# An attention kernel on TensorE: context matmuls of 256 columns, one head each, and the heads of the g tensors 64 bytes further apart in SBUF

## The chip, the cores and the metric

The kernel runs on one core of one Trainium2 chip. The metric is the device time of one execution in microseconds (us), the median of three runs. SBUF is the on-chip memory of 128 partitions from which TensorE reads both operands of a matmul; PSUM is the one that it writes.

## The reference

Cross attention with 8 heads over 8 batches, 256 queries, 256 keys and head width 256, then a projection, a residual and a layer norm:

```python
Q = (img_embed @ Wq).reshape(B, -1, H, D).transpose(0, 2, 1, 3)
K = (sent_embed @ Wk).reshape(B, -1, H, D).transpose(0, 2, 1, 3)
V = (sent_embed @ Wv).reshape(B, -1, H, D).transpose(0, 2, 1, 3)
score = jnp.einsum('bhqd,bhkd->bhqk', Q, K) / math.sqrt(D)
score = jnp.where(mask, score, -jnp.inf)
attn = jax.nn.softmax(score, axis=-1)
ctx = jnp.einsum('bhqk,bhkd->bqhd', attn, V).reshape(B, -1, H * D)
out = ctx @ Wo + img_embed
# then (out - mean) / sqrt(var + 1e-05) * gamma + beta over the last axis
```

`img_embed` is x (8, 256, 256) and `sent_embed` is ctx_768 (8, 256, 192), both float32.

## The kernel before, in words

Once, at the start, the weights are folded per head: A = Wq Wk^T (256 x 192, `fold_A`, L324) and C = Wv Wo (192 x 256, `fold_C`, L341). Scores are then x A ctx^T, and the output is the sum over heads of (attn ctx) C. The 192 context features are split in a lower part of 128 (tensors with L) and an upper part of 64 (U); the upper parts of two heads share one tile of 128 partitions.

Every product on TensorE is made of float32r matmuls on operands split in two: a hi part (the value rounded to float32r by ScalarE, `hi_part`) and a lo part (the rest, by VectorE or GpSimd, `lo_part`); the products hi*hi, hi*lo and lo*hi are accumulated in PSUM.

The work goes in 32 steps (8 batches of 4 head pairs; `t` is the step, `j` the pair, `b` the batch). TensorE's own order in one step (`step`, L501) is:

1. `scores(t)`, L383: 20 matmuls of 256 columns, head 0's ten and then head 1's ten. Stationary operand: a 128-column slice of `gL_hi`, `gL_lo` or `gU`; moving operand: `ctxT_hi` or `ctxT_lo`.
2. `query_products(t + 1)`, L365: 18 of 256 columns. Stationary `A_hi`, `A_lo`; moving `xT_hi`, `xT_lo`. They fill `gU_bank` and `gL_bank`, from which ScalarE and VectorE make the g tensors of the next step.
3. `output_products(t - 4)`, L458 to L499: 18 of 256 columns. Stationary `tL_hi`, `tL_lo`, `tU_hi`, `tU_lo`; moving `CL_*`, `CU_*`.
4. `context_products(t - 3)`, L420: 10 matmuls of 512 columns, both heads in one. Stationary `ctxL_hi`, `ctxL_lo`, `ctxU`; moving `pT_hi`, `pT_lo` (the transposed probabilities).

Each matmul has a weight load of its own (LDWEIGHTS) ahead of it, also where the next one uses the same stationary slice. Steps 6 to 29 run in a hardware loop of four steps; the others are written out. In the first steps, in which there is nothing yet for parts 3 and 4, `fold_C` stands in their place. In the last steps the order is written out by hand: the probabilities of steps 30 and 31 are transposed on TensorE (`transposes`, L405), and step 30 keeps its t tensors elsewhere (`places`, L133): tL in `xT_hi`/`xT_lo`, tU in the two halves of `gU`.

All engines work from in-order queues. ScalarE takes the exponentials and the hi parts, VectorE the row maxima, lo parts and 32x32 transposes, GpSimd the normalisation and the lo part of pT, SyncE the DMAs. Semaphores tie them together: `g_hi_done` and `g_split` release the scores, `pT_hi_done` and `pT_split` the context phase, `t_product` (raised when tL and when tU are complete) releases ScalarE's `t_hi_part`.

**Where the operands lie.** SBUF tensors are laid one behind the other in the order in which the program declares them, each rounded up to 32 bytes per partition. Up to `tU_lo` all sizes are multiples of 256 bytes, and the first tensor starts at a multiple of 128. Then come `eps_col` and `power_col` (8 bytes each, 32 taken), then the g tensors, xT, ctxT, C and pT. So, in bytes modulo 128, A, ctxL, ctxU, tL and tU start at 0, and gL, gU, xT, ctxT, CL, CU and pT at 64. Slices of 128 columns are 512 bytes long, and every slice that a matmul reads starts a multiple of 256 bytes into its tensor.

Of the kernel before, what the change touches and what calls it, by code (L numbers as in the profile page):

```python
# [8 lines left out]
F32R = mybir.dt.float32r  # L9
# [4 lines left out]
P = 128  # L14
B = 8
S = 256
# [12 lines left out]
KT = KV // P  # L29
# [7 lines left out]
SQ = 32  # L37
SQUARES = KV // SQ
ROWS = P // SQ

def attention_kernel(nc, xT, x, ctxT, ctx, mask, wqT, wkT, wvT, wo, gamma, beta, out, scratch):
    es = ExitStack()
    with es:
        def sb(name, shape, dt=F32):
            return es.enter_context(nc.sbuf_tensor(name, shape, dt))
# [14 lines left out]
        ctxL_hi = sb("ctxL_hi", [P, KT, P], F32R)  # L60
# [7 lines left out]
        eps_col = sb("eps_col", [P, QT])  # L68
        power_col = sb("power_col", [P, QT])

        gL_hi = sb("gL_hi", [P, 2, S], F32R)
        gL_lo = sb("gL_lo", [P, 2, S], F32R)
        gU = sb("gU", [P, 2, S], F32R)

        xT_hi = sb("xT_hi", [P, IT, S], F32R)
        xT_lo = sb("xT_lo", [P, IT, S], F32R)
# [239 lines left out]
        def _(pe):  # L316
            def split_products(into, pairs, first=True, last=True, shared=False):

                for n, (stationary, moving) in enumerate(pairs):
                    ins = nc.tensor.matmul(into, stationary, moving, start=first and n == 0,  # L320
                                           stop=last and n == len(pairs) - 1, skip_group_check=shared)
                return ins
# [97 lines left out]
            def context_products(t, j, b):  # L420

                if j == 0:

                    pe.wait_ge(C_split, 2 * (PAIRS - 1))

                    pe.wait_ge(ctx_split, 2 * b + 2)
                hi, lo, tL, tU = pT_hi[j % 2], pT_lo[j % 2], places("tL", t)[0], places("tU", t)[0]

                pe.wait_ge(pT_hi_done, 2 * t + 2)
                if isinstance(t, int) and t == STEPS - 1:  # L430

                    split_products(tU[:], [(ctxU[:, k, :], hi[:, k]) for k in range(KT)], last=False)
                    pe.wait_ge(pT_split, 2 * t + 2)
                    split_products(tU[:], [(ctxU[:, k, :], lo[:, k]) for k in range(KT)],
                                   first=False).then_inc(t_product, 1)
                    split_products(tL[:], [pair for k in range(KT) for pair in
                                           [(ctxL_hi[:, k, :], hi[:, k]), (ctxL_lo[:, k, :], hi[:, k]),
                                            (ctxL_hi[:, k, :], lo[:, k])]]).then_inc(t_product, 1)
                    return
                split_products(tL[:], [(part[:, k, :], hi[:, k]) for k in range(KT) for part in (ctxL_hi, ctxL_lo)],  # L440
                               last=False)

                if isinstance(t, int) and STEPS - 4 <= t < STEPS - 2:

                    pe.wait_ge(tU_summed, 2 * t)
                split_products(tU[:], [(ctxU[:, k, :], hi[:, k]) for k in range(KT)], last=False)
                by_squares = not (isinstance(t, int) and t >= STEPS - 2)
                for k in range(KT):

                    pe.wait_ge(pT_split, 2 * t + (k + 1 if by_squares else 2))  # L450
                    end = k == KT - 1
                    lower = split_products(tL[:], [(ctxL_hi[:, k, :], lo[:, k])], first=False, last=end)
                    if end:
                        lower.then_inc(t_product, 1)
                    upper = split_products(tU[:], [(ctxU[:, k, :], lo[:, k])], first=False, last=end)
                upper.then_inc(t_product, 1)

            def output_lower(t, j, b, q):  # L458
# [665 lines left out]
```

## Time and profile before

| | |
|---|---|
| median of three runs | 319.12 us (319.02 to 319.21) |
| the profiled execution | 319.14 us |
| its span, first to last instruction | 317.3 us |
| matmuls recorded | 2264 |
| PE (matmul) busy | 309.8 us |
| PEld (weight load) busy | 290.7 us |
| VectorE (DVE) busy | 253.0 us |
| ScalarE (ACT) busy | 221.9 us |
| GpSimd (POOL) busy | 181.2 us |
| mean granted TensorE clock | 0.998 of full speed |

The profile and its trace are of one execution. Engines are named as in the table. Matmuls overlap in the pipeline, so the duration of one (0.28 us for 256 columns) is longer than what it takes of the engine's time; that is read from the distance between the starts of consecutive matmuls, here called the pitch. The timeline has starts to 0.01 us, so a pitch is taken over many matmuls. L320 is the line of the helper `split_products` that issues all matmuls of the four phases; the phases are told apart by their tiles.

### The profile page before, as it was taken

To read this page: it belongs to the slowest core of one execution; us is meant where nothing else is said; L and a number is where in the kernel's file an instruction comes from. 1 tells how busy PE (TensorE), PEld (TensorE's weight loads), DVE (VectorE), ACT (ScalarE), POOL (GpSimd) and SP (SyncE) were. 2 spreads that over 40 slices of the span, in tenths; PEclk is the share of its full clock that TensorE was granted. 3 is DMA by queue.
4 is the path that set the end of the run, shared out by engine and by line. 5 is a ranking of instruction groups with operands and counts; after the bars stand their busy time and mean duration, and the time that the engine had idled before them with its cause. 6 is when DMAs were issued, how large, how long until landed. Compare 5 with 4: busy or idle time off the path is not lost.

```text
span 317.3 us, 7411 instructions
## 1 busy us (share of the span) xinstructions
PE 309.8 (98%) x2264; PEld 290.7 (92%) x2264; DVE 253.0 (80%) x721; ACT 221.9 (70%) x601; POOL 181.2 (57%) x183
## 2 busy tenths in 40 slices
PE   8899999999999999999999999999999999999993
PEld 7898888999999999999999999999999999999982
DVE  0466778777999879987998889987998889975686
ACT  2446677768867787678777797678767887777640
POOL 1123476457864587558855586558755686457312
PEclk9999999999999999999999999999999999999999
DMA  7995443464344553484446444364356435440101
GB/s 257 365 409 219 136 155 130 141 211 136 99 146 169 189 166 121 140 243 136 132 128 198 156 154 158 131 215 150 115 190 180 169 101 186 144 138 20 35 0 66
DMA packets 46910, 50.26 MB, mean 158 GB/s; under 512 B 3504, under 2 KB 37040, under 8 KB 46896
## 3 DMA queue, kind: packets, MB, share of 16 engines
q1 hardware_dynamic: 46608, 49.56, 47.2%
q10 hardware_dynamic: 288, 0.52, 0.6%
q8 instruction: 7, 0.11, 0.2%
q14 instruction: 7, 0.06, 0.1%
HBM read 32.24 MB, written 17.83 MB: 158 GB/s over the span
## 4 chain that ended last, share of the span: by engine, by line
PE 93%; DMA 2%; DVE 2%; ACT 1%; SPq 1%; issue 0%; POOLq 0%; POOL 0%; DVEq 0%
PE score_bank L320 25%; PE out_bank L320 19%; PE gL_bank L320 14%; PE tL_bank L320 13%; PE tU_bank L320 9%; PE gU_bank L320 7%; DMA wq_raw<-in_wqT 2%; PE spare_bank L354 1%; PE tL_bank L354 1%; PE spare_bank L320 1%; PE tL_bank L336 1%; PE tU_bank L336 1%; PE out_bank L360 1%; PE tU_bank L360 1%; DVE tU L827 1%; PE out_bank L336 0%
## 5 line engine op out<-in xcount | busy, mean ns | idle before, releaser
L1003 POOL TENSOR_TENSOR probs<-probs,inv_sum 128x512 f32<-128x512 f32 x64 | 66.6, 1041 | 85.5 <-DVE inv_sum L790 84.9
L601 ACT ACTIVATE probs<-neg_scores,neg_max 128x256 f32<-128x256 f32 x128 | 64.2, 503 | 35.5 <-DVE neg_max L779 35.4
L1026 POOL TENSOR_TENSOR pT_lo<-pT_raw,pT_hi 128x512 fp32r<-128x512 f32 x60 | 76.5, 1297 | 8.6 <-ACT pT_hi L558 8.6
L779 DVE CUSTOM_DVE_ANT_0 neg_scores<-score_bank,mask_bias 128x256 f32<-128x256 f32 x128 | 49.1, 420 | 6.5 <-PE score_bank L320 4.0
L800 DVE STREAM_TRANSPOSE squares<-probs 128x512 f32<-128x512 f32 x60 | 42.3, 706 | 0.5 <-DMA scratch<-squares 0.2
L558 ACT ACTIVATE tL_hi<-tL_bank 128x512 fp32r<-128x512 f32 x31 | 18.5, 598 | 31.5 <-PE tL_bank L320 31.5
L320 PE MATMUL score_bank<-ctxT_hi,gU 128*128 128x256 f32 x128 | 36.5, 285 | 0.0
L727 DVE TENSOR_TENSOR tL_lo<-tL_bank,tL_hi 128x512 fp32r<-128x512 f32 x31 | 21.4, 689 | 18.8 <-ACT tL_hi L558 18.8
L320 PE MATMUL score_bank<-ctxT_hi,gL_lo 128*128 128x256 f32 x128 | 36.2, 283 | 0.0
L320 PE MATMUL score_bank<-ctxT_hi,gL_hi 128*128 128x256 f32 x128 | 36.2, 283 | 0.0
L320 PE MATMUL score_bank<-ctxT_lo,gL_hi 128*128 128x256 f32 x128 | 36.2, 283 | 0.0
L320 PE MATMUL score_bank<-ctxT_lo,gU 128*128 128x256 f32 x128 | 36.2, 283 | 0.0
L320 PE MATMUL gL_bank<-xT_hi,A_hi 128*128 128x256 f32 x128 | 35.3, 276 | 0.0
L320 PE MATMUL gL_bank<-xT_lo,A_hi 128*128 128x256 f32 x128 | 35.3, 276 | 0.0
L320 PE MATMUL gL_bank<-xT_hi,A_lo 128*128 128x256 f32 x128 | 35.3, 276 | 0.0
L558 ACT ACTIVATE pT_hi<-pT_raw 128x512 fp32r<-128x512 f32 x60 | 34.3, 622 | 0.0
L320 PE MATMUL out_bank<-CL_lo,tL_hi 128*128 128x256 f32 x118 | 32.6, 276 | 0.0
L320 PE MATMUL out_bank<-CL_hi,tL_hi 128*128 128x256 f32 x118 | 32.6, 276 | 0.0
L320 PE MATMUL out_bank<-CL_hi,tL_lo 128*128 128x256 f32 x118 | 32.6, 276 | 0.0
L727 DVE TENSOR_TENSOR gU<-gU_bank,gU 64x256 fp32r<-64x256 f32 x64 | 27.0, 423 | 2.1
L827 DVE TENSOR_TENSOR tU<-tU_bank,tU_moved 64x256 f32<-64x256 f32 x62 | 26.0, 419 | 1.6 <-ACT tU_moved L642 0.6
L320 PEld LDWEIGHTS score_bank<-ctxT_hi,gU 128*128 128x128 f32 x128 | 24.4, 191 | 2.6 <-issue 1.2
(167 smaller groups left out, 946.8 us busy)
## 6 DMA issues: line engine op xcount, KB each, us to landing
scratch<-squares SPq DMA_DIRECT2D x30, 512.0 KB, 2.7
pT_raw<-scratch SPq DMA_DIRECT2D x120, 128.0 KB, 3.1
xT_raw<-in_xT SPq DMA_DIRECT2D x8, 256.0 KB, 4.5
ctxT_raw<-in_ctxT SPq DMA_DIRECT2D x8, 256.0 KB, 4.7
wo_raw<-in_wo SPq DMA_DIRECT2D x4, 512.0 KB, 13.7
x_res<-in_x SPq DMA_DIRECT2D x8, 256.0 KB, 3.2
out<-y_out SPq DMA_DIRECT2D x7, 256.0 KB, 2.8
wq_raw<-in_wqT SPq DMA_DIRECT2D x3, 512.0 KB, 7.6
```

The source lines that it names most:

```text
L320: ins = nc.tensor.matmul(into, stationary, moving, start=first and n == 0, stop=last and n == len(pairs) - 1, skip_group_check=shared)
L336: ins = nc.tensor.matmul(dst[:, i * DL:(i + 1) * DL], wq_raw[:, h * DT + d, i * P:(i + 1) * P], wk_raw[:, h * DT + d, :], start=d == 0, st ...
L354: ins = nc.tensor.matmul(lower[:, hh, :], wv_raw[:, h * DT + d, 0:P], wo_raw[:, h * DT + d, :], start=d == 0, stop=d == DT - 1)
L360: ins = nc.tensor.matmul(upper[hh * UP:(hh + 1) * UP, 0, :], wv_raw[:, h * DT + d, P:DL], wo_raw[:, h * DT + d, :], start=d == 0, stop=d = ...
L558: return nc.scalar.activation(dst, src, ACT.Copy)
L601: nc.scalar.activation(probs[j % 2][:, n, :], neg_scores[:, n, :], ACT.Exp, bias=neg_max[:, n:n + 1], scale=-1.0, accum_out=row_sum[:, n:n ...
L727: return nc.vector.tensor_tensor(dst, whole, hi.bitcast(F32), ALU.subtract)
L779: nc.vector.tensor_tensor_reduce(out=neg_scores[:, n, :], in0=score_bank[hh][:, q, :], in1=mask_bias[:], scale=-SCALE, scalar=3.0e38, op0= ...
L800: nc.vector.transpose(squares[:, :, rows, :].rearrange("p s n c -> p n s c"), probs[j % 2][:, rows, :].rearrange("p n (s c) -> p n s c", c ...
L827: nc.vector.tensor_tensor(tU[part, :], places("tU", t)[0][part, hh, :], tU_moved[part, :], ALU.add).then_inc(tU_summed, 1)
L1003: nc.gpsimd.tensor_tensor(probs[j % 2][:, rows, :], probs[j % 2][:, rows, :], inv, ALU.mult) \
L1026: nc.gpsimd.tensor_tensor(pT_lo[j % 2][:, k].rearrange("p hh (q i r) -> p (hh q) i r", q=QT, i=ROWS), pT_raw[j % 2][:, k].rearrange("p i n ...
```

## The change

The g tensors get 16 float32 of padding behind each head, so that head 1 starts 1088 instead of 1024 bytes behind head 0, and each of the three takes 128 bytes more. And the context phase issues for each (stationary, moving) pair two matmuls of 256 columns, one for each head, instead of one of 512. The two write their own halves of the PSUM bank; only the first of a bank carries the start flag. Order of pairs, waits and semaphore increments are as before.

```diff
+APART = 16
@@
-        gL_hi = sb("gL_hi", [P, 2, S], F32R)
-        gL_lo = sb("gL_lo", [P, 2, S], F32R)
-        gU = sb("gU", [P, 2, S], F32R)
+        gL_hi = sb("gL_hi", [P, 2, S + APART], F32R)[:, :, 0:S]
+        gL_lo = sb("gL_lo", [P, 2, S + APART], F32R)[:, :, 0:S]
+        gU = sb("gU", [P, 2, S + APART], F32R)[:, :, 0:S]
@@
+                def halves(into, stationary, moving, first=False, last=False):
+
+                    for hh in range(2):
+                        ins = split_products(into[:, hh, :], [(stationary, moving[:, hh, :])],
+                                             first=first and hh == 0, last=last, shared=True)
+                    return ins
+
                 pe.wait_ge(pT_hi_done, 2 * t + 2)
                 if isinstance(t, int) and t == STEPS - 1:
...
-                split_products(tL[:], [(part[:, k, :], hi[:, k]) for k in range(KT) for part in (ctxL_hi, ctxL_lo)],
-                               last=False)
+                for k in range(KT):
+                    halves(tL, ctxL_hi[:, k, :], hi[:, k], first=k == 0)
+                    halves(tL, ctxL_lo[:, k, :], hi[:, k])
 
                 if isinstance(t, int) and STEPS - 4 <= t < STEPS - 2:
 
                     pe.wait_ge(tU_summed, 2 * t)
-                split_products(tU[:], [(ctxU[:, k, :], hi[:, k]) for k in range(KT)], last=False)
+                for k in range(KT):
+                    halves(tU, ctxU[:, k, :], hi[:, k], first=k == 0)
                 by_squares = not (isinstance(t, int) and t >= STEPS - 2)
                 for k in range(KT):
 
                     pe.wait_ge(pT_split, 2 * t + (k + 1 if by_squares else 2))
                     end = k == KT - 1
-                    lower = split_products(tL[:], [(ctxL_hi[:, k, :], lo[:, k])], first=False, last=end)
+                    lower = halves(tL, ctxL_hi[:, k, :], lo[:, k], last=end)
                     if end:
                         lower.then_inc(t_product, 1)
-                    upper = split_products(tU[:], [(ctxU[:, k, :], lo[:, k])], first=False, last=end)
+                    upper = halves(tU, ctxU[:, k, :], lo[:, k], last=end)
                 upper.then_inc(t_product, 1)
```

The branch for the last step is changed in the same way. Since the three g tensors are 384 bytes longer together, all that lies behind them (xT, ctxT, C, pT) moves up by 384 bytes, three times 128. In bytes modulo 128 the streams (xT, ctxT, C, pT) stay at 64, head 0 of the g tensors stays at 64, and head 1 comes to lie at 0, as A, ctx and t do.

## Rows read from the trace of the kernel before

**Rows 1.** The page, parts 1 and 4: busy time; the chain that ended last, by engine

```profile
PE 309.8 (98%) x2264; PEld 290.7 (92%) x2264; DVE 253.0 (80%) x721; ACT 221.9 (70%) x601; POOL 181.2 (57%) x183
PE 93%; DMA 2%; DVE 2%; ACT 1%; SPq 1%; issue 0%; POOLq 0%; POOL 0%; DVEq 0%
```

**Rows 2.** Timeline of PE in the loop: start us, duration us, engine, line, operation, out<-in

```profile
103.74 0.28 PE L320 MATMUL score_bank<-ctxT_hi,gU 128*128 128x256 f32 x1
...
106.14 0.28 PE L320 MATMUL gU_bank<-xT_hi,A_hi 128*128 128x256 f32 x1
...
108.18 0.28 PE L320 MATMUL out_bank<-CL_hi,tL_hi 128*128 128x256 f32 x1
...
110.22 0.39 PE L320 MATMUL tL_bank<-pT_hi,ctxL_hi 128*128 128x512 f32 x1
...
112.50 0.28 PE L320 MATMUL score_bank<-ctxT_hi,gU 128*128 128x256 f32 x1
...
138.78 0.28 PE L320 MATMUL score_bank<-ctxT_hi,gU 128*128 128x256 f32 x1
```

**Rows 3.** Groups of matmuls by form: shapes, count | busy us, mean ns | idle before

```profile
L320 PE MATMUL score_bank<-ctxT_hi,gL_hi 128*128 128x256 f32 x128 | 36.2, 283 | 0.0
...
L320 PE MATMUL gL_bank<-xT_hi,A_hi 128*128 128x256 f32 x128 | 35.3, 276 | 0.0
...
L320 PE MATMUL out_bank<-CL_hi,tL_hi 128*128 128x256 f32 x118 | 32.6, 276 | 0.0
...
L320 PE MATMUL out_bank<-CL_hi,xT_hi 128*128 128x256 f32 x2 | 0.6, 283 | 0.0
```

**Rows 4.** Timeline of PE, output products of step 30, from xT and gU

```profile
307.29 0.28 PE L320 MATMUL spare_bank<-CL_hi,xT_hi 128*128 128x256 f32 x1
307.40 0.28 PE L320 MATMUL spare_bank<-CL_lo,xT_hi 128*128 128x256 f32 x1
307.52 0.28 PE L320 MATMUL spare_bank<-CL_hi,xT_lo 128*128 128x256 f32 x1
...
309.32 0.28 PE L320 MATMUL out_bank<-CU_hi,gU 128*128 128x256 f32 x1
```

**Rows 5.** Timeline of PE, ordinary output products in two places of the tail

```profile
293.74 0.28 PE L320 MATMUL out_bank<-CU_hi,tU_hi 128*128 128x256 f32 x1
...
294.33 0.28 PE L320 MATMUL out_bank<-CU_hi,tU_lo 128*128 128x256 f32 x1
...
310.04 0.28 PE L320 MATMUL spare_bank<-CL_hi,tL_lo 128*128 128x256 f32 x1
...
311.80 0.28 PE L320 MATMUL out_bank<-CU_hi,tU_lo 128*128 128x256 f32 x1
```

**Rows 6.** Timeline of PE, from the context phase of step 30 to that of step 31

```profile
302.02 0.40 PE L320 MATMUL score_bank<-pT_hi,ctxL_hi 128*128 128x512 f32 x1
...
304.32 0.28 PE L320 MATMUL spare_bank<-CU_hi,tU_hi 128*128 128x256 f32 x1
...
305.00 0.62 PE L320 MATMUL tU_bank<-pT_hi,ctxU 128*128 128x512 f32 x2
```

**Rows 7.** Timeline of PE, scores and query products behind fold_C, before any context phase

```profile
26.62 0.39 PE L320 MATMUL score_bank<-ctxT_hi,gU 128*128 128x256 f32 x1
...
27.47 0.28 PE L320 MATMUL score_bank<-ctxT_lo,gU 128*128 128x256 f32 x1
...
28.06 0.28 PE L320 MATMUL score_bank<-ctxT_lo,gU 128*128 128x256 f32 x1
...
29.14 0.28 PE L320 MATMUL gU_bank<-xT_hi,A_hi 128*128 128x256 f32 x1
...
31.07 0.28 PE L320 MATMUL gL_bank<-xT_hi,A_lo 128*128 128x256 f32 x1
```

**Rows 8.** Timeline of VectorE and GpSimd in the step of rows 2

```profile
110.57 0.69 DVE L727 TENSOR_TENSOR gL_lo<-gL_bank,gL_hi 128x512 fp32r<-128x512 f32 x1
...
103.63 1.29 POOL L1026 TENSOR_TENSOR pT_lo<-pT_raw,pT_hi 128x512 fp32r<-128x512 f32 x1
```

More of the change, by code:

```diff
@@ L433, in context_products @@
                     pe.wait_ge(pT_split, 2 * t + 2)
[L434 to L438, printed above, removed]
+                    for k in range(KT):
+                        upper = halves(tU, ctxU[:, k, :], lo[:, k], last=k == KT - 1)
@@ L439, in context_products @@
+                    upper.then_inc(t_product, 1)
+                    for k in range(KT):
+                        halves(tL, ctxL_hi[:, k, :], hi[:, k], first=k == 0)
+                        halves(tL, ctxL_lo[:, k, :], hi[:, k])
+                        lower = halves(tL, ctxL_hi[:, k, :], lo[:, k], last=k == KT - 1)
+                    lower.then_inc(t_product, 1)
                     return
-                split_products(tL[:], [(part[:, k, :], hi[:, k]) for k in range(KT) for part in (ctxL_hi, ctxL_lo)],
-                               last=False)
+                for k in range(KT):
+                    halves(tL, ctxL_hi[:, k, :], hi[:, k], first=k == 0)
+                    halves(tL, ctxL_lo[:, k, :], hi[:, k])
@@ L443, in context_products @@
                 if isinstance(t, int) and STEPS - 4 <= t < STEPS - 2:
                     pe.wait_ge(tU_summed, 2 * t)
-                split_products(tU[:], [(ctxU[:, k, :], hi[:, k]) for k in range(KT)], last=False)
+                for k in range(KT):
+                    halves(tU, ctxU[:, k, :], hi[:, k], first=k == 0)
                 by_squares = not (isinstance(t, int) and t >= STEPS - 2)
```

## The prediction

> **What bounds the kernel now.** I read first the page's busy times and its chain: PE is busy 98% of the span and holds 93% of the chain; no other engine's busy share is above 80% [rows 1]. So the time is TensorE's, and the question is what each matmul takes of it. Durations don't tell that, since matmuls overlap, so I went to the timeline of one loop step and took pitches, start to start [rows 2]. Scores: 103.74 to 106.14 is 2.40 us for 20 matmuls, 0.120 each. Query products: 2.04 us for 18, 0.1133 each. Output products: the same. Context: 110.22 to 112.50 is 2.28 us for 10 of 512 columns, 0.228 each. A step is 8.76 us, and four steps take 138.78 - 103.74 = 35.04 us, so the next four repeat it: no loop iteration loses anything at its branch.
>
> Two oddities carry the argument. First, 256 columns cost 0.1133 us in two phases and 0.120 in a third. Second, 512 columns cost 0.228, not less than twice 0.1133 = 0.2267. The first shows in the groups by form as well: score matmuls last 283 ns, query and output ones 276 [rows 3]. What is different about scores? The same table has the answer: the output products whose stationary operand is `xT_hi` (step 30) last 283 too, while the same products from `tL_hi` last 276, with the same moving tensor `CL_hi`. In the timeline the former settle at 0.120: from 307.52 to 309.32, 15 pitches in 1.80 us, where the products from gU are among them [rows 4]. So the slow pitch goes with where the stationary operand lies: scores (g against ctxT) and these (xT or gU against C) have both operands at 64 modulo 128, and A, ctx and t, at 0, meet streams at 64. I call the two cases "same place" and "apart".
>
> There is a third gait. Behind a context phase or a gap, products with operands apart can go at 0.118: 293.74 to 294.33 is 0.59 us for 5 pitches, and 310.04 to 311.80 is 1.76 for 15, which is 0.117 [rows 5]. TensorE keeps this gait until something changes it. What changes it is a run at the same place: behind a fold (gap at 26.62) the scores are at 0.120 from 28.06 on (1.08 us for 9), and the query products behind them then run at 1.93 / 17 = 0.1135 [rows 7]. In the loop it is the same: 0.120, and then 36 pitches of 0.1133 [rows 2].
>
> **The change part by part.**
>
> Head 1's scores, 10 of the 20 in each step, go from same place to apart. I take for them the pitch of the query products that follow a run of scores, 0.1133. This saves 10 x (0.1200 - 0.1133) = 0.067 us a step, 2.13 us over 32 steps. Bounds for head 1's pitch: 0.1133 (nothing with operands apart is faster in the trace) and 0.120 (no effect, 0 us); 0.118, the third gait, would save only 0.6 us. I take 0.1133 because every switch from a settled 0.120 to operands apart in the trace gives it at once [rows 2, 7]. Is head 0's run of ten long enough to settle? Coming from a context phase, the tail shows pitches of 0.11, 0.12 and then 0.120 throughout [rows 4], so ten are plenty in the loop. Behind a fold, the pace is still irregular up to the seventh matmul and beyond [rows 7]; steps 0 to 3 may therefore put head 1 and the query products of one or two steps at 0.118, 28 x 0.0045 = 0.13 us each. I count nothing and keep 0.26 for the range.
>
> Why 64 bytes should matter modulo 128, while the streams also move by 384 bytes against A, t and ctx, is not shown by any row: all pairs in the trace are 0 or 64 apart modulo 512. A hint in the numbers: 256 columns at the granted 2.4 GHz are 106.7 ns, so 0.1133 is 16 columns more and 0.120 is 32 more; 16 float32 columns are 64 bytes. Losses in pieces of 64 bytes and a distance of 64 bytes that decides make two alternating places, a period of 128, the simplest reading. It is an estimate, and its failure is a rival below.
>
> The context phase: 20 x 0.1133 = 2.267 against 2.287 (2.28 in the rows, the timeline being cut to 0.01; ten times the mean over a loop step, 8.76 - 2.39 - 4.08 = 2.29). That saves 0.02 us a step. The halves of pT lie at 64, as C and xT do, and ctx at 0, as A and t, so the pair is one that the trace has 36 times per step. Bounds: 0.1133, and 0.118 (2.36, a loss of 0.07). I take 0.1133, as the phase is entered at that pitch and nothing in it is at the same place. Steps 0 to 28 give 29 x 0.02 = 0.58 us. The six output products behind step 28's context no longer fall to 0.118, 0.03 more. But in the tail the transposes leave TensorE in the slow gait, and there the 512-column phase was what ended it. Step 30's context took 2.30 us, the six products behind it 0.68, step 31's 307.29 - 305.00 = 2.29 [rows 4, 6]; if all stay at 0.1177 these are 2.35, 0.71 and 2.35. With the same for step 29 (0.08) the tail gives back 0.05 + 0.03 + 0.06 + 0.08 = 0.22 us. The context phases together: -0.58 - 0.03 + 0.22 = -0.39 us.
>
> The rule of the Trainium skill that speaks against this part is a fixed cost per matmul. The rows say no: a fixed cost would make 512 columns cheaper than two of 256, and they are not [rows 2]. The page "TensorE: Matmul & The Clock Gate" (Back-to-back issue gap) puts the warm gap at N/2.4 + 2.5 ns, by which splitting would cost 10 x 2.5 ns a step, and 0.8 us in all. The trace has 0.228 us for 512 columns where that formula has 0.216, so its constant doesn't hold here.
>
> Weight loads and issue: ten more loads and matmuls a step. A load lies beside the stream of the matmul ahead of it, now 0.113 us long instead of 0.228; 56 of 66 matmuls already have such a cover with 0.0 idle [rows 2, 3]. The branch and the register instructions of the loop are covered by queued matmuls, and there are 56 pairs in a row at the short pitch without a gap [rows 2]. Cost 0; were the queue to run dry, the loop branch would show as a gap of up to some 0.3 us in six places, which I don't expect.
>
> The other engines: the earliest data that TensorE needs is `gL_lo`, done at 110.57 + 0.69 = 111.26, used behind 112.50: over 1.2 us of slack, against 0.09 by which the step shrinks. The pT lo part ends at 104.92 and is used at 110.22 or later [rows 2, 8]. Both chains start from TensorE's products and move up with them. tL and tU are complete at the same place of the phase. The padding makes the g tiles two rows of 256 for ScalarE and VectorE instead of one of 512, at worst some tens of ns inside that slack.
>
> Sum: -2.13 - 0.39 = -2.52 us. The profiled execution took 319.14 (span 317.3 and 1.8 around it), the median is 319.12. Forecast 316.6 us; span 314.8; a loop step 8.76 - 0.067 - 0.020 = 8.67 us. With the start (up to +0.26), the tail (-0.22 if it doesn't stay slow) and 0.01 on a context phase each way (0.3), this case alone reaches from 316.1 to 317.2.
>
> **The rivals.**
>
> *The address has nothing to do with it, or not in this way.* Scores stay at 0.120 for both heads: 319.1 - 0.4 = 318.7. For: the two slow kinds might share something else. Against: 283 and 276 ns for the same products that differ in the stationary tensor alone [rows 3]. The same page (Step-by-step, the part on LDWEIGHTS) says that loading the next weights doesn't take SBUF read bandwidth from the running matmul, which is this rival as a rule; the rows just named speak against it.
>
> *The slow gait in the loop (slower than before).* If a run of ten at the same place no longer resets TensorE, the 66 other matmuls of a step go at 0.1177: 1.19 + 7.77 = 8.96 us, 0.20 more than 8.76; over some 31 steps +6.2, 325.3 us. It decides as soon as head 1 leaves at 0.118 instead of 0.113. Against: 0.120 is reached by the third matmul in rows 4.
>
> *The period is longer than 128 bytes.* Then two things are open. Both heads may get away from their stream (head 0's three tensors are 384, 256 and 128 bytes from it modulo 512): 20 x 0.0067 x 32 = 4.3 us saved, 314.5. Or the 56 others, which now stand 448 instead of 64 from their streams, take the 0.120 pitch: 36 x 0.0067 + (2.40 - 2.29) = +0.35 us a step, 11 us in all, less what the scores bring: 326 to 330.
>
> **How the numbers follow.** Forecast case 0.74. Address without effect, 318.7: 0.10. Slow gait, 325: 0.06. Longer period, gain (314.5) 0.05, loss 0.05. The range 316.1 to 318.9 takes in the first two, 0.84. A measurement of this kernel can't tell less than 0.2% (0.64 us) from no change: 318.7 is "same" (0.10), the forecast and the larger gain are "faster" (0.79), the rest "slower" (0.11).
>
> **What would show it.** In the loop, head 1's ten scores should span 1.13 us and head 0's 1.19; twenty context matmuls 2.27; four steps 34.7. The groups by form of the scores should split in two pitches, and their mean durations fall from 283 to about 280 ns. Query and output pitches must stay at 0.1133; 0.118 there means the slow gait, 0.120 a longer period. Head 1 at 0.120 means that the address is not the cause.

## The result, and the profile after

The changed kernel takes 317.94 us (median of seven, 317.86 to 318.27) against 319.13 us (319.02 to 319.38): a ratio of 0.9963, 95% interval 0.9951 to 0.9974. It is faster by 1.2 us, where 2.5 were forecast. The profiled execution has a span of 316.1 us at a granted clock of 0.997, against 317.3.

The page of the changed kernel, busy times and chain [rows 1]:

```profile
PE 309.5 (98%) x2584; PEld 303.4 (96%) x2584; DVE 253.1 (80%) x721; ACT 222.0 (70%) x601; POOL 181.3 (57%) x183
...
PE 95%; DMA 2%; DVE 1%; SPq 1%; POOLq 0%; issue 0%; POOL 0%
```

320 more matmuls and loads, the other engines unchanged, PE bounds it as before. The timeline of PE in a loop step, and the start of the fourth step behind it [rows 2]:

```profile
103.37 0.28 PE L321 MATMUL score_bank<-ctxT_hi,gU 128*128 128x256 f32 x1
...
104.55 0.28 PE L321 MATMUL score_bank<-ctxT_hi,gU 128*128 128x256 f32 x1
...
105.72 0.28 PE L321 MATMUL gU_bank<-xT_hi,A_hi 128*128 128x256 f32 x1
105.84 0.28 PE L321 MATMUL gU_bank<-xT_lo,A_hi 128*128 128x256 f32 x1
105.96 0.28 PE L321 MATMUL gU_bank<-xT_hi,A_lo 128*128 128x256 f32 x1
...
107.78 0.28 PE L321 MATMUL out_bank<-CL_hi,tL_hi 128*128 128x256 f32 x1
...
109.81 0.28 PE L321 MATMUL tL_bank<-pT_hi,ctxL_hi 128*128 128x256 f32 x1
...
112.09 0.28 PE L321 MATMUL score_bank<-ctxT_hi,gU 128*128 128x256 f32 x1
...
138.25 0.28 PE L321 MATMUL score_bank<-ctxT_hi,gU 128*128 128x256 f32 x1
```

Four steps take 138.25 - 103.37 = 34.88 us, 8.72 each: 0.04 less than before, where 0.09 was forecast. The parts: head 0's scores 1.18 us, head 1's 1.17 (before 2.40 together), query products 2.06, output products 2.03, context 2.28 to the cut of the timeline. From the starts in ns, averaged over the loop: scores 2.355 instead of 2.393, query 2.054 instead of 2.040, output 2.040 in both, context 2.271 instead of 2.287. Two things don't fit the forecast. Head 1's pitch is 0.117, not 0.1133; and the first query products behind it have 0.12 (105.72, 105.84, 105.96) before they go at 0.1133. Head 0's is not a flat 0.120 but irregular, from 0.112 to 0.128 (0.118 on average). In two early steps, 2 and 4, the forecast did come true, head 1's ten scores at 0.113, and the query products behind them at 0.113 from the first one; step 2:

```profile
35.26 0.28 PE L321 MATMUL score_bank<-ctxT_hi,gU 128*128 128x256 f32 x1
...
36.39 0.28 PE L321 MATMUL gU_bank<-xT_hi,A_hi 128*128 128x256 f32 x1
```

The groups by form [rows 3] (shapes, count | busy us, mean ns | idle):

```profile
L321 PE MATMUL score_bank<-ctxT_hi,gU 128*128 128x256 f32 x128 | 36.1, 282 | 0.0
...
L321 PE MATMUL score_bank<-ctxT_hi,gL_hi 128*128 128x256 f32 x128 | 35.6, 278 | 0.0
...
L321 PE MATMUL gL_bank<-xT_hi,A_hi 128*128 128x256 f32 x128 | 35.3, 276 | 0.0
...
L321 PE MATMUL out_bank<-CL_hi,xT_hi 128*128 128x256 f32 x2 | 0.6, 283 | 0.0
```

The score groups fell from between 283 and 285 ns to between 278 and 282; the query products of gL stay at 276, the first of gU (`xT_hi`, `A_hi`) rose from 278 to 282, and products from `xT_hi` stay at 283. The tail, context phase of step 30, six output products, context phase of step 31 [rows 6]:

```profile
300.81 0.28 PE L321 MATMUL score_bank<-pT_hi,ctxL_hi 128*128 128x256 f32 x1
...
303.16 0.28 PE L321 MATMUL spare_bank<-CU_hi,tU_hi 128*128 128x256 f32 x1
...
303.87 0.28 PE L321 MATMUL tU_bank<-pT_hi,ctxU 128*128 128x256 f32 x1
...
306.22 0.28 PE L321 MATMUL spare_bank<-CL_hi,xT_hi 128*128 128x256 f32 x1
```

2.35, 0.71 and 2.35 us, to the hundredth what was worked out for a slow gait that stays. The scores of step 30 start at 286.49 us instead of 287.70; all of the gain has been made by then, and what follows takes 29.6 us in both kernels. The 0.23 us that the slow gait costs there come back almost whole in other places of the tail: 0.05 in and behind the context phase of step 28, and 0.16 in the last 36 output products (4.79 us before, 4.63 after), where the wait for the products of step 31 is 0.09 us shorter and what follows it goes at 0.114 instead of 0.118.

### The profile page after: what moved, and what is told of

The parts are those of the page before. It is cut to its first block, busy times and chain, and to the rows that moved or that the text cites. A ratio compares the mean times of both kernels' runs of the same rounds, so it can differ in the third digit from the quotient of the medians.

```text
span 316.1 us, 8051 instructions
## 1 busy us (share of the span) xinstructions
PE 309.5 (98%) x2584; PEld 303.4 (96%) x2584; DVE 253.1 (80%) x721; ACT 222.0 (70%) x601; POOL 181.3 (57%) x183
## 4 chain that ended last, share of the span: by engine, by line
PE 95%; DMA 2%; DVE 1%; SPq 1%; POOLq 0%; issue 0%; POOL 0%
PE score_bank L321 25%; PE out_bank L321 19%; PE gL_bank L321 14%; PE tL_bank L321 13%; PE tU_bank L321 9%; PE gU_bank L321 7%; DMA wq_raw<-in_wqT 2%; PE spare_bank L321 1%; PE tL_bank L355 1%; PE spare_bank L355 1%; PE tL_bank L337 1%; PE tU_bank L337 1%; PE out_bank L361 1%; PE tU_bank L361 1%; PE out_bank L337 0%; PE spare_bank L337 0%
## 5 line engine op out<-in xcount | busy, mean ns | idle before, releaser
L572 ACT ACTIVATE tL_hi<-tL_bank 128x512 fp32r<-128x512 f32 x31 | 18.6, 599 | 29.6 <-PE tL_bank L321 29.6
```

Of the source, the lines that this page charges most:

```text
L572: return nc.scalar.activation(dst, src, ACT.Copy)
```

## The experiments

**How the layouts are told.** The distance of a stationary operand from its stream is given modulo 256 bytes, for a reason that e5 shows: 0 is the same place, -64 stands 64 bytes behind, +64 ahead, and 128 is opposite. Of head 0 and 1 the three tensors `gL_hi`, `gL_lo`, `gU` stand in this order; "A" means A, ctx and t. "Halves" is the context phase in 20 matmuls as in the change. "Good" is a pitch of 0.1133 us, "slow" 0.1177.

| kernel | head 0 | head 1 | A | context | loop step, us | total, us | ratio |
|---|---|---|---|---|---|---|---|
| before | 0 | 0 | -64 | 512 | 8.760 | 319.13 | |
| changed | 128, 0, 128 | -64, +64, -64 | +64 | halves | 8.720 | 317.94 | 0.9963 |
| e1 | 128, 0, 128 | -64, +64, -64 | +64 | 512 | 8.800 | 320.36 | 1.0033 |
| e2 | 0 | 0 | -64 | halves | 8.747 | 319.43 | 1.0000 |
| e3 | 0 | +64 | -64 | halves | 8.973 | 325.5 | 1.0192 |
| e4 | 128 | 128 | -64 | 512 | 8.913 | 323.66 | 1.0134 |
| e6 | +64 | +64 | -64 | halves | 8.953 | 324.63 | one run |
| e9 | 0 | -64 | -64 | halves | 8.973 | 325.46 | 1.0195 |
| e10 | 128, 0, 128 | -64 | -64 | halves | 8.973 | 325.22 | 1.0208 |
| e11 | 0 | -64, +64, -64 | -64 | halves | 8.680 | 317.18 | 0.9940 |
| e12 | 0 | -64 | -64 | 512 | 8.693 | 317.34 | 0.9944 |
| e13 | -64, +64, -64 | -64, +64, -64 | -64 | halves | 8.613 | 315.71 | 0.9887 |
| e15 | -64 | -64 | -64 | halves | 8.951 | 324.81 | 1.0168 |
| e16 | -64, +64, -64 | -64, +64, -64 | -64 | 512 | 8.887 | 322.9 | 1.0114 |
| e17 | 0 | 0 | +64 | 512 | 8.953 | 324.84 | 1.0172 |
| e18 | 128, 0, 128 | -64, +64, -64 | -64 | halves | 8.98 | 325.45 | 1.0192 |

Ten of these sixteen totals lie near 317 or near 325 us, and which of the two is a matter of whether the 0.1177 gait survives the scores.

**The two parts of the change alone.** e1 has the padding only, e2 the halves only (the change with `APART = 0`).

```diff
+APART = 16
 ...
-        gL_hi = sb("gL_hi", [P, 2, S], F32R)
+        gL_hi = sb("gL_hi", [P, 2, S + APART], F32R)[:, :, 0:S]
 ... (gL_lo and gU in the same way)
```

> The padding of the g tensors alone; the context phase keeps its 10 matmuls of 512 columns. Three theories on why head 1's scores took 0.117 us each in the changed kernel and not 0.1133. T1, run too short: ten matmuls at the same place don't settle at 0.120, and without that TensorE leaves them in the slow gait. T2, period: head 0's three g tensors lie 384, 256 and 128 bytes from their stream modulo 512, not 0 as before, and only 0 is the same place. T3, entry: a context phase of 256-column matmuls hands over in another state than one of 512. T1 and T2 expect the same ragged scores here (2.355 us per step, against 2.39 before), T3 expects head 0 settled at 0.120 and head 1 at 0.1133, 2.327 us. Time: T1 and T2 318.0 to 318.2 us, T3 317.0.

> The context phase of 20 matmuls of 256 columns alone; the padding is 0, so all g tensors lie as before. T1 and T2 expect scores at 0.120 as before from the third on (2.39 us), context 2.27 us, a step of 8.74 us and 318.6 us in all (0.58 us gained in the loop, 0.2 given back in the tail). T3 expects the scores ragged, 0.117 or so each.

Measured: padding alone 320.36 us, a ratio of 1.0033 (1.0020 to 1.0045), slower; halves alone 319.43, 1.0000 (0.9990 to 1.0009). So neither part brings anything alone, and the change isn't a sum of two. In e1 head 1's scores take what they take in the changed kernel (1.173 us), and head 0's 0.025 more (1.209), but the context phase has gone from 2.287 to 2.324 us, in pitches of 0.226 once and then 0.236 and 0.231 in turn. The 512-column phase is hurt by the new layout and the halves (2.271) are not. In e2 the context takes 2.267 us, as worked out, and a loop step 0.013 less than before. But the scores of step 30 start only 0.03 us earlier than before. Step 4 starts 0.10 us later and takes 8.99 us instead of 8.76: its twenty scores at the same place, entered at 0.118, go 0.121, 0.120, 0.124, 0.117, 0.118 and again, and query, output and context products behind them all at 0.118. The next step's run becomes a steady 0.120 from its seventh pitch on, and 0.1133 follows. That, and the tail, is what the loop's gain went into; the forecast of e2, 318.6, was missed by it.

**Is the period 128 or 256?** e3 is the changed kernel with fillers behind each g tensor, so that all three heads 0 are at their stream's place by any period and the streams keep their own residue. e4 is the kernel before with the whole g block 128 bytes further on. e5 adds to the kernel before, at its end, groups of 20 matmuls whose stationary slice starts at growing distances from the stream, each behind twelve at the same place; their results are not used.

```diff
 e3:     gL_hi = sb("gL_hi", [P, 2, S + APART], F32R)[:, :, 0:S]
+        sb("fill0", [P, S - 2 * APART])
 ... (the same behind gL_lo and gU)
 e4:
+        sb("ahead", [P, 32])
         gL_hi = sb("gL_hi", [P, 2, S], F32R)
 ...
+        sb("behind", [P, 224])
 e5:
+            flat = CL_hi[:].rearrange("p h c -> p (h c)")
+            for off in OFFSETS:
+                for _ in range(12):
+                    nc.tensor.matmul(score_bank[0][:, 0, :], flat[:, 0:P], flat[:, 256:512], start=True, stop=True)
+                for _ in range(20):
+                    nc.tensor.matmul(score_bank[1][:, 0, :], flat[:, off:off + P], flat[:, 256:512], start=True, stop=True)
 ... (and once more, each behind six small matmuls of 128 columns)
```

> The changed kernel with a filler of 896 bytes behind each padded g tensor, so that head 0 of all three and all streams lie where they lay before modulo 1024, and head 1 is 64 bytes further. T2: head 0 settles at 0.120 by its third matmul, head 1 goes at 0.1133: scores 2.327 us, a step 8.67 us, 316.7 us in all. T1 and T3: as in the changed kernel, scores 2.355 us, 317.9 us.

> The kernel before, with 128 bytes ahead of the g tensors and 896 behind them: all score pairs are 384 bytes apart modulo 512 and 0 modulo 128, everything else lies as before. A period of 128 expects all scores at 0.120 and the time of the kernel before, 319.1 us. T2, a longer period, expects another pitch for the scores: ragged or 0.1133, and 317 to 318 us.

> The kernel before with a measurement behind its last matmul (its results unused): for 16 distances between a 128-column stationary slice and a 256-column stream of the same tensor, 20 matmuls at that distance behind 12 at a distance of 1024 bytes, and then again 20 behind six short float32 matmuls. Distance in bytes modulo 1024, stationary ahead of its 1024-byte place: 0, 16, 32, 48, 64, 80, 96, 128, 160, 192, 256, 320, 384, 448, 512, 768. A period of 128 expects 0.120 at 0, 128, 256, 384 and 512 and 0.1133 at 64, 192, 320. A longer period expects 128 (and perhaps 256) to differ from 0. Two gaits with a memory expect a distance of 64 to run at 0.1133 in the first set and at 0.1177 in the second, and 0 to run at 0.120 in both.

e4, which would be the kernel before if the period were 128, takes 323.66 us (1.0117 to 1.0151): head 0's scores go at 0.1176, head 1's at 0.1185 in a pattern of five, and the 36 products behind them at 0.1178. In e5, the timeline of PE; L560 are the 20 at an offset of 0, 64, 128, 256 and 320 bytes, and the row behind each is the first of the next twelve:

```profile
313.29 2.56 PE L560 MATMUL score_bank<-CL_hi 128*128 128x256 f32 x20
315.69 0.29 PE L558 MATMUL score_bank<-CL_hi 128*128 128x256 f32 x1
...
328.53 2.52 PE L560 MATMUL score_bank<-CL_hi 128*128 128x256 f32 x20
330.89 0.28 PE L558 MATMUL score_bank<-CL_hi 128*128 128x256 f32 x1
...
339.92 2.53 PE L560 MATMUL score_bank<-CL_hi 128*128 128x256 f32 x20
342.29 0.28 PE L558 MATMUL score_bank<-CL_hi 128*128 128x256 f32 x1
...
351.35 2.56 PE L560 MATMUL score_bank<-CL_hi 128*128 128x256 f32 x20
353.75 0.29 PE L558 MATMUL score_bank<-CL_hi 128*128 128x256 f32 x1
...
355.20 2.44 PE L560 MATMUL score_bank<-CL_hi 128*128 128x256 f32 x20
357.47 0.28 PE L558 MATMUL score_bank<-CL_hi 128*128 128x256 f32 x1
```

2.40, 2.36, 2.37, 2.40 and 2.27 us for twenty: 0.120, 0.118, 0.1186, 0.120, 0.1135. The offsets of 512 and 768 bytes gave 0.120 as well, 384 gave 0.1186. So the same place comes back every 256 bytes, and 128 is a kind of its own. (One other offset, 160 bytes, gave 0.120 too.) And distances of 64 bytes give the good or the slow pitch at the same residue: 0.1135 at 320 and 448 bytes, 0.118 at 64 and 192. Behind a gap and small float32 matmuls all four were slow. Address alone doesn't set it; what ran before does too.

e3 is the forecast's own picture made exact, and it is 1.9% slower than before (1.0175 to 1.0209). Its loop step:

```profile
105.37 0.28 PE L324 MATMUL score_bank<-ctxT_hi,gU 128*128 128x256 f32 x1
...
106.57 0.28 PE L324 MATMUL score_bank<-ctxT_hi,gU 128*128 128x256 f32 x1
...
107.75 0.28 PE L324 MATMUL gU_bank<-xT_hi,A_hi 128*128 128x256 f32 x1
...
109.87 0.28 PE L324 MATMUL out_bank<-CL_hi,tL_hi 128*128 128x256 f32 x1
...
111.99 0.40 PE L324 MATMUL tL_bank<-pT_hi,ctxL_hi 128*128 128x256 f32 x2
...
114.34 0.28 PE L324 MATMUL score_bank<-ctxT_hi,gU 128*128 128x256 f32 x1
```

Head 0 1.20 us at the same place, and then everything at 0.118: query 2.12, output 2.12, context 2.35. A run of ten at the same place didn't end the slow gait. Head 0's ten were in a ragged form there, 0.121, 0.120, 0.124, 0.117, 0.118 and again, with the same mean as the flat 0.120 of the kernel before.

**Is the slow gait one that stays?** e6 puts all scores at +64; e7 adds to it, in step 5, ten matmuls of `xT_hi` against itself (same place, unused results); e8 is e3 with the same ten.

```diff
 e6:
+        sb("ahead", [P, 16])
         gL_hi = sb("gL_hi", [P, 2, S], F32R)
 ...
 e7 (on e6), e8 (on e3):
+                if isinstance(t, int) and t == RESET_AT:
+                    for _ in range(RESET):
+                        nc.tensor.matmul(spare_bank[:, 0, :], xT_hi[:, 0, 0:P], xT_hi[:, 0, :], start=True, stop=True)
```

> Context phase in halves as in the changed kernel; the g tensors unpadded, but all three moved by 64 bytes, so that both heads are apart from their streams and the streams lie as before modulo 1024. Nothing in the loop is at the same place. If the gait has a memory and only a run at the same place ends the slow one, the whole loop goes at 0.1177: a step of 8.95 us, some 325 us in all. If the good gait comes by itself: 8.61 us a step, 315 us.

> The same with ten extra matmuls at the same place (xT against itself, result unused), once, in step 5. Memory: from step 5 on everything goes at 0.1133, a step is 8.61 us; 25 steps gain 0.147 each, the first steps and the tail stay slow, the extra run costs 1.2: 316.5 to 317 us, below the changed kernel. Without memory: as the kernel without the extra run.

> The kernel of e3 (head 0 exactly where it was, head 1 64 bytes off, 8.973 us a step) with the same ten extra matmuls in step 5. If head 0's ten scores settle at 0.120 when they are entered in the good gait, the loop holds it: head 0 1.19, head 1 1.13, a step 8.67 us, 318 us in all. If ten are too few however they are entered, the loop falls back to 8.97 us a step and the time stays at 325 us.

e6: 324.63 us, every pitch of the loop at 0.1177. e7: four executions of 316.76 to 317.25 and one of 325.04; the ratio is that of the four, 0.9924 (0.9908 to 0.9941). So ten extra matmuls early on, 1.2 us of work, save 7.5 us against the one execution of e6; and in e7's own trace query products go at 0.118 in step 4 and at 0.1133 behind the ten. The gait is a state that lasts. The profiled execution is the one of 325.04, and it shows how the good gait ended, at a granted clock of 1.0. All pitches are 0.113 from the ten matmuls on until this place in step 9; the first row is VectorE's:

```profile
96.03 0.69 DVE L747 TENSOR_TENSOR gL_lo<-gL_bank,gL_hi 128x512 fp32r<-128x512 f32 x1
...
96.76 0.28 PE L324 MATMUL score_bank<-ctxT_lo,gL_hi 128*128 128x256 f32 x1
96.87 0.29 PE L324 MATMUL score_bank<-ctxT_hi,gL_lo 128*128 128x256 f32 x1
97.00 0.28 PE L324 MATMUL score_bank<-ctxT_hi,gU 128*128 128x256 f32 x1
97.12 0.28 PE L324 MATMUL score_bank<-ctxT_lo,gU 128*128 128x256 f32 x1
```

One pitch of 0.129 (96.87 to 97.00), and 0.118 from there on. The profile reports no idle time, but a wait stands in the kernel at just this matmul: the fifth score of a step is the first to read `gL_lo`, behind a wait for `g_split`. VectorE completed `gL_lo` at 96.72, only 0.15 us before that matmul started. This holds in all the traces: of 640 fifth scores in the twenty traces, 17 have a pitch above 0.126 us (0.127 to 0.226), and these are exactly the 17 whose `gL_lo` was complete 0.15 us or less ahead of them. They lie in steps 1, 3 and 9. So the single long pitches are TensorE waiting for VectorE's `gL_lo`, and what it has to spare in step 9 shrinks as the steps ahead get shorter: 0.38 us before, 0.23 in e14, 0.14 in e13.

e8: 326.28 us (1.0201 to 1.0236), no gain. The rows show the ten, and step 6:

```profile
62.63 1.36 PE L527 MATMUL spare_bank<-xT_hi 128*128 128x256 f32 x10
63.83 0.28 PE L326 MATMUL gU_bank<-xT_hi,A_hi 128*128 128x256 f32 x1
...
70.18 0.28 PE L326 MATMUL score_bank<-ctxT_hi,gU 128*128 128x256 f32 x1
...
71.37 0.28 PE L326 MATMUL score_bank<-ctxT_hi,gU 128*128 128x256 f32 x1
...
72.55 0.28 PE L326 MATMUL gU_bank<-xT_hi,A_hi 128*128 128x256 f32 x1
```

Behind the ten, the query, output and context products of step 5 are good. Then head 0 of step 6 is flat (1.19 us), and head 1, at +64, is at 0.118 at once (1.18) and all behind it too.

**The side.** Is it the side on which the next operands stand? e9 puts head 1 at -64, e12 is e9 with the context in 512 columns, e14 is e9 with the ten matmuls in step 5.

```diff
 e9:
-        gL_hi = sb("gL_hi", [P, 2, S + APART], F32R)[:, :, 0:S]
+        gL_hi = sb("gL_hi", [P, 2, S + 48], F32R)[:, :, 0:S]
+        sb("fill1", [P, 32])
 ... (gL_lo and gU in the same way)
```

> What the runs before this one point to: places repeat every 256 bytes (0, 256, 512 and 768 alike, 128 and 384 unlike them), and behind a run at the same place a stationary operand 64 bytes behind its stream takes the good gait, one 64 bytes ahead of it the slow one. Here head 0 of the three g tensors lies at its streams' place modulo 256, as before, and head 1 is 192 bytes further, which is 64 bytes behind its streams modulo 256, as A, ctx and t are. Context in halves. The side theory expects head 0 at 0.120 (1.19 us), head 1 at 0.1133 (1.13 us), no slow gait in the loop, a step of 8.67 us and 316.6 to 316.9 us. If only the length of the run at the same place matters, ten are too few here as in e3, and it is 325 us.

> As e9, but the context phase keeps its 10 matmuls of 512 columns. If the halves are worth their 0.013 to 0.02 us a step and no more, a step is 8.69 us and the time 316.9 us; if the phase of 512 columns hands over in a state from which head 0's ten don't settle, as the padding alone did (e1), the time is above 319 us.

> e9 (8.973 us a step) with ten extra matmuls at the same place (xT against itself) in step 5. If e9's two forms are only a matter of entry, head 0 is flat at 0.120 and head 1 at 0.1133 from step 6 on: a step 8.68 us, some 318.4 us with the extra run and the slow steps 4 and 5. In e8, with head 1 on the other side, the same run didn't help. If ten are too few in any case: 8.97 us, 326 us.

e9 alone missed: 325.46 us, slow in the loop. But in its steps 0 to 3 head 1 ran at 0.113 behind a head 0 that had come to 0.120; the first context phase, behind the gap that a fold leaves, went at 0.118, met a ragged head 0 (51.10, 51.22, 51.34, 51.47, 51.58), and nothing ended it again. With the 512-column phase (e12) 317.34 us (0.9929 to 0.9959), and with the ten (e14) 318.63 (0.9966 to 0.9987), in both head 1 at 1.133 us in every loop step. So e8 and e14 differ, modulo 256 bytes, in head 1's side alone: ahead, it turned slow behind the first flat run; behind, it stayed good for all the loop. It is no rule for every place: the offset of 320 bytes in e5 stands ahead, behind a ragged run, and went at 0.1135.

**Head 1 and head 0 of the changed kernel, each in the surroundings of before.** e11 has head 1 as changed with head 0 in line; e10 has head 0 as changed with head 1 at -64.

```diff
 e11:
+        gL_hi = sb("gL_hi", [P, 2, S + 48], F32R)[:, :, 0:S]
+        sb("fill1", [P, 32])
+        gL_lo = sb("gL_lo", [P, 2, S + 16], F32R)[:, :, 0:S]
 ... (gU as gL_hi)
 e10:
+        sb("fill0", [P, 32])
+        gL_hi = sb("gL_hi", [P, 2, S + 16], F32R)[:, :, 0:S]
+        gL_lo = sb("gL_lo", [P, 2, S + 48], F32R)[:, :, 0:S]
 ... (gU as gL_hi)
```

> As e9, but head 0 lies to its streams as in the changed kernel modulo 256 (gL_hi and gU 128 away, gL_lo at the same place), head 1 all 64 behind. If head 0's unequal places are what costs in the changed kernel: head 0 ragged (1.18 us) and head 1 not at 0.1133, about 317.9 us. If it is head 1's mixed sides: head 1 at 1.13 to 1.14 us, a step 8.67 us, 316.7 us.

> As e9, but head 1 lies to its streams as in the changed kernel modulo 256 (gL_hi and gU 64 behind, gL_lo 64 ahead), head 0 all at the same place. If head 1's mixed sides are what costs: head 1 at 1.17 us, the first query products slow, 317.9 us. If it is head 0's places: head 1 at 1.13 us, 316.7 us.

e11: 317.18 us (0.9925 to 0.9955); starts at 103.29, 104.49 and 105.63 give head 0 1.20 and head 1 1.14, the pitch that was forecast. It even left the slow gait inside head 1 of step 4 (0.118 three times, then 0.116, 0.114, 0.113). e10: 325.22, slow in the whole loop, though head 1 went at 0.113 in its steps 0, 2 and 3. By itself e10 doesn't accuse head 0, since e9, which has head 0 in line and the same head 1, is just as slow. The pair that differs in head 0 alone is e11 and e18 (below): 317.18 against 325.45 us. So with A behind its stream it is head 0 of the change, opposite in two tensors of three, that spoils the run, and not head 1. With A ahead, as the changed kernel has it, no run puts head 0 in line under a padded head 1.

**All scores off their stream's place.** e13 and e15 move the g tensors by fillers alone: in e13 `gL_hi` and `gU` at -64 and `gL_lo` at +64, in e15 all at -64. e16 is e13's layout with the context in 512 columns.

```diff
 e13:
+        sb("fill0", [P, 48])
         gL_hi = sb("gL_hi", [P, 2, S], F32R)
+        sb("fill1", [P, 32])
         gL_lo = sb("gL_lo", [P, 2, S], F32R)
+        sb("fill2", [P, 32])
         gU = sb("gU", [P, 2, S], F32R)
+        sb("fill3", [P, 144])
```

> Context in halves. No score at the same place: in both heads gL_hi and gU lie 64 bytes behind their streams modulo 256, gL_lo 64 bytes ahead; no padding. If the mixture of sides ends the slow gait, as head 1 of e11 suggests, the loop goes at 0.1133 throughout: scores 2.27 us, a step 8.61 us, some 315 us in all. If only a run at the same place can end it, the loop stays at 0.1177: 8.95 us a step, 325 us.

> As e13, but all three g tensors lie 64 bytes behind their streams, as A, ctx and t do: one side only in the whole loop, nothing at the same place. The mixture theory expects that nothing ends the slow gait in which step 4 enters: 8.95 us a step, 325 us. If the slow gait ends by itself where all distances are the same: 8.61 us, 315 us.

> The layout of e13 (all scores mixed, nothing at the same place) with the context phase of 10 matmuls of 512 columns. If the scores are at 0.1133 here too and the context takes 2.287 us, a step is 8.63 us, 0.02 more than in e13, and the time 316.0 to 316.3 us. If the 512-column phase hands over in the slow gait and the scores have to end it in each step, a step is 8.65 to 8.70 us, 316.8 to 318.4 us. Sent as well: nothing else; e13 is compared through the kernel before.

e13 is the fastest, 315.71 us, 0.9887 (0.9871 to 0.9904). Its timeline, in the step behind another single long pitch (0.140, at 94.85):

```profile
103.35 0.28 PE L324 MATMUL score_bank<-ctxT_hi,gU 128*128 128x256 f32 x1
...
103.93 0.28 PE L324 MATMUL score_bank<-ctxT_hi,gU 128*128 128x256 f32 x1
...
105.63 0.28 PE L324 MATMUL gU_bank<-xT_hi,A_hi 128*128 128x256 f32 x1
...
111.98 0.28 PE L324 MATMUL score_bank<-ctxT_hi,gU 128*128 128x256 f32 x1
...
137.82 0.28 PE L324 MATMUL score_bank<-ctxT_hi,gU 128*128 128x256 f32 x1
```

The first five scores are still slow (0.58 us), the other fifteen take 1.70, 0.1133 each: the mixture ended the gait here, and in step 4 too. It didn't in steps 0 to 3, nor in the step of the long pitch itself, whose last fifteen stayed at 0.118 on average. The three steps from 111.98 to 137.82 take 25.84 us, 8.613 each. e15, without a tensor on the other side, never leaves the gait. e16 missed what I expected of the mixture: 322.9 us, query and output at 0.118. With the 512-column phase ahead of it the same mixture doesn't end the gait, so there is no rule "mixed heads recover".

**The other side of A.** In the changed kernel the streams have moved 384 bytes and A, ctx and t haven't. e17 moves g and all streams of the kernel before by 128 bytes and changes nothing else; e18 has both heads as changed, and A where it was.

```diff
 e17:
+        sb("ahead", [P, 32])
         gL_hi = sb("gL_hi", [P, 2, S], F32R)
 ...
 e18:
+        sb("fill0", [P, 32])
         gL_hi = sb("gL_hi", [P, 2, S + 16], F32R)[:, :, 0:S]
         gL_lo = sb("gL_lo", [P, 2, S + 16], F32R)[:, :, 0:S]
         gU = sb("gU", [P, 2, S + 16], F32R)[:, :, 0:S]
+        sb("fill3", [P, 128])
```

> The kernel before with a tensor of 128 bytes a partition put ahead of g, so that g and all streams move 128 bytes together: every score is still at its stream's place (0 mod 256 apart), but A, the context and t, which stood 64 bytes behind their streams, now stand 64 bytes ahead of them. Theory that the side of these matters (a flat run of 0.120 hands over to a good run when what follows stands 64 behind, to a slow one when it stands 64 ahead, as e8 against e14): query and out products slow, 0.118, context 2.31 to 2.36, a loop step of 8.9 to 8.97 us, total 324 to 326 us. Theory that only the scores' places matter: a loop step of 8.76, total 319.1 us.

> Heads 0 and 1 of g stand to their streams exactly as in the changed kernel (head 0: gL_hi and gU 128 away, gL_lo at the same place; head 1: gL_hi and gU 64 behind, gL_lo 64 ahead), context in halves, but A, the context and t stay 64 bytes behind their streams as in the kernel before, where the changed kernel has them 64 ahead. If the side of A, context and t does not matter: 8.72 us a step, total 317.9 us. If it does: more than 0.02 us a step away from that, with the difference in the query products and the scores behind them (8.61 to 8.68, 316 to 317 us, or slow, 8.95, 325 us).

e17: 324.84 us, 1.0172 (1.0155 to 1.0189). A loop step, both heads and the query products:

```profile
105.58 0.28 PE L321 MATMUL score_bank<-ctxT_hi,gU 128*128 128x256 f32 x1
...
106.76 0.28 PE L321 MATMUL score_bank<-ctxT_hi,gU 128*128 128x256 f32 x1
...
107.95 0.28 PE L321 MATMUL gU_bank<-xT_hi,A_hi 128*128 128x256 f32 x1
...
110.07 0.28 PE L321 MATMUL out_bank<-CL_hi,tL_hi 128*128 128x256 f32 x1
```

Head 1 goes flat at 0.120 (1.19 us for ten), and the 18 query products behind it take 2.12 us instead of 2.04. In the kernel before, the same run hands over to 0.1133 [rows 2]. Nothing in the program differs but the side. Head 0 is at its stream's place here too, and yet takes 1.178 us, irregular from 0.112 to 0.121. e18: 325.45 us, 1.0192 (1.0175 to 1.0209). It was good in steps 1 and 2; then, in step 3, a single long pitch came (`gL_lo` 0.13 us ahead of its matmul), and the query products of that step no longer recover:

```profile
42.16 0.31 PE L322 MATMUL score_bank<-ctxT_hi,gL_lo 128*128 128x256 f32 x1
42.31 0.28 PE L322 MATMUL score_bank<-ctxT_hi,gU 128*128 128x256 f32 x1
...
44.07 0.28 PE L322 MATMUL gU_bank<-xT_hi,A_hi 128*128 128x256 f32 x1
44.19 0.28 PE L322 MATMUL gU_bank<-xT_lo,A_hi 128*128 128x256 f32 x1
```

42.16 to 42.31 is 0.148 us; behind head 1 the query products go at 0.118 (44.07, 44.19) and stay there. In the changed kernel, with A ahead, two pitches of 0.12 are followed by 0.1133 in every step. The 384 bytes, counted at nothing, are what separates 317.9 from 325.5 here.

## Why the prediction was half right

**What bounds the kernel** was right, and so was the reading of three pitches and of where they come from. "Address has no effect" is refuted by e4, e17 and e13: they differ from before in fillers, and e13 in the halves, which alone change nothing (e2). They take 323.66, 324.84 and 315.71 us. The rule by which the load of the next weights takes nothing from the running matmul (the Trainium skill, "TensorE: Matmul & The Clock Gate", Step-by-step) doesn't foretell these 2.9%. No run shows what in the chip is shared.

**The step that failed is head 1's pitch of 0.1133 us behind head 0's run, and one premise of it is the period of 128 bytes.** The period rested on a remark about 16 columns and on no row, since all pairs of the kernel before were 0 or 64 apart. e5 has the same place every 256 bytes. The forecast took head 0 as unchanged, with 384 bytes between its streams and A as nothing. By 256, two of its three tensors are opposite their stream. It runs irregular, at 0.118, and doesn't hand over the good gait (e18 against e11, which differ in head 0 alone). The other premise is that a settled run at the same place gives 0.1133 at once; e3 has the forecast's picture by any period, and took 325.5 us.

**The term that was too large is head 1's:** 0.067 us a step forecast, 1.200 - 1.171 = 0.029 measured, a pitch of 0.1171 and not 0.1133. The mechanism for head 1 exists, with exactly the size forecast, in e11 and e12 (1.133), where head 0 is flat. In the changed kernel head 1 goes near the slow pitch, and the query products pay 0.014 more. Head 0 gained 0.009 that I didn't count. Together 0.024 a step instead of 0.067, some 1.3 us less over 31 steps: nearly all that is missing. Of the signs named ahead, the twenty context matmuls in 2.27 us came; head 1 in 1.13 and four steps in 34.7 didn't (1.17 and 34.88). That 317.94 lies within the stated range is no merit of the case forecast: the range reached up to the rival without an effect, and the time fell between the two.

**"A run at the same place resets TensorE"** was too wide a reading of [rows 2, 7]. The run has a flat and a ragged form with one mean. In the loops the flat one handed over to 0.1133 where the next operands stand behind their stream (before, e14), and not where they stand ahead (e8, e17); behind the ragged one the loops of e3 and e9 and step 4 of e2 stayed slow. The offset of 320 bytes in e5 fits neither half. The rows of before had one form and one side.

**The rival "slow gait in the loop"** was priced right, 8.96 us and 325.3, and seven kernels landed there (8.95 to 8.98, 324.6 to 325.5). It even got the layout that the forecast described, e3. The changed kernel missed it because A had changed sides (e18). The forecast's sign was thus right by luck, by a distance that it had called nothing; 0.06 was too small a chance.

**The context term** was right: 0.016 a step of 0.020, and 2.35, 0.71 and 2.35 us in the tail. That fixed costs per matmul are nothing held, as e2's 2.267 shows. But the halves aren't neutral in a given layout: they bring 2.4 us beside the change's padding (e1), 7 us beside e13's (e16), and lose 8 beside e9's (e12). The scores are entered differently behind the two forms (head 0 begins with 0.113 in e12 and 0.121 in e9); why, no run shows.

**The slack of `gL_lo`** was read from one step, 1.2 us. The same kernel before has 0.38 us in step 9 and 0.13 in step 1. Where the steps ahead of step 9 took 8.61 us instead of 8.76, it fell to 0.14 (e13) and 0.15 (e7), and there the good gait ended.

**Left open:** the rule by which a run picks its gait. Distance, side and the form of the run before all enter, and no single one of them foretells e10, e13 and e16. Nor is it known why one late `gL_lo` is followed by the slow gait in e7 and e13 and not in e14 (step 3, 0.127 us). No run gives `gL_lo` more time to test it.

## What to carry to other kernels

Where TensorE bounds a kernel, read start-to-start pitches phase by phase, not durations or busy shares: at about 98% busy, 315.7 and 325.5 us were both to be had from the same matmuls. Write down the distance of each stationary operand from its stream modulo 256 bytes before and after a change of the layout, for all tensors behind the one that is edited. Look at the data that arrives just in time as well: a wait that costs 0.02 us by itself stood ahead of a slower gait for the rest of the program (e7). And look for a layout that regains the fast gait in every step, over one that merely keeps it once it is there.

## What the runs showed of the hardware

Float32r matmuls of 256 columns at a granted clock of 0.995 to 1.0 ran at three steady pitches, 0.1133, 0.1177 and 0.120 us. A distance of 0 modulo 256 bytes gave 0.120 on average at the offsets 0, 256, 512 and 768 of e5 and in most loops, though 0.1178 in head 0 of e17. 0.1133 and 0.1177 are two states at the same addresses, and either held for over 180 us at a stretch (slow from 97 us to the end in e7, good from 104 to 293 us in e13). Ten matmuls whose results nobody used made the program 7.5 us faster (four of five executions of e7 against the one of e6). Moving operands by 128 bytes cost 5.5 us (e17). A matmul whose operand was complete 0.15 us or less before it had a pitch of 0.127 to 0.226 us instead of 0.113 to 0.124 (17 cases of 640), and in one execution of e7 such a pitch, 16 ns longer, stands at the change from 0.113 to 0.118; that execution took 8 us longer than the others.
